# Two heads of the first layer's output projection as a block product in seven parts

## What is computed

```python
h_q = (rmsnorm(layernorm(x)) @ w_q.T).reshape(8, 128, 32, 128)   # 32 heads of 128
h_k = (context @ w_k.T).reshape(8, 128, 32, 128)
h_v = (context @ w_v.T).reshape(8, 128, 32, 128)
score = softmax(einsum("bqhd,bkhd->bhqk", h_q, h_k) + position_bias, masked)
attn = einsum("bhqk,bkhd->bqhd", score, h_v).reshape(8, 128, 4096)
x = x + tanh(gate) * (layernorm(x) + attn @ w_out.T)
```

## Time and profile before

| what | value |
|---|---|
| runs | 1004.22, 1004.27, 1004.35 us |
| the profiled execution: its time, its span | 1004.49 us, 1002.7 us |
| PE, DVE, ACT, POOL busy | 99%, 47%, 41%, 34% of the span |
| one group, from output projection to output projection | 105.1 us |
| output projection, all groups | 768 matmuls of 512 columns, 180.6 us busy |

### The profile page before, as it was taken

How to read it: one execution, slowest core, us unless ns; L and a number is a source line. 1 busy time by engine, 2 the same in 40 slices (tenths; PEclk the granted TensorE clock), 3 DMA queues, 4 the chain that set the end, 5 groups by cost and what they waited for, 6 DMA issues and landing times.

```text
span 1002.7 us, 14920 instructions
## 1 busy us (share of the span) xinstructions
PE 995.0 (99%) x5204; PEld 844.5 (84%) x5204; DVE 466.8 (47%) x957; ACT 413.2 (41%) x1110; POOL 336.4 (34%) x317
## 2 busy tenths in 40 slices
PE   8999999999999999999999999999999999999998
PEld 7888888888888888888888888888888888888885
DVE  5654622462155305532364235622462287766664
ACT  6563233432453244334442344234432454555630
POOL 3351414122330424041414051314122333587640
PEclk9999999999999999999999999999999999999999
DMA  8021111101110201010111011111101103300002
GB/s 312 22 84 55 42 43 64 32 21 63 42 52 0 84 28 55 10 63 21 63 31 63 21 63 31 42 42 63 31 21 64 42 2 99 122 33 1 1 1 84
DMA packets 16402, 50.52 MB, mean 50 GB/s; under 512 B 3056, under 2 KB 3312, under 8 KB 15600
## 3 DMA queue, kind: packets, MB, share of 16 engines
q1 hardware_dynamic: 15360, 48.75, 14.2%
q10 hardware_dynamic: 1008, 1.32, 0.4%
HBM read 47.97 MB, written 2.10 MB: 50 GB/s over the span
## 4 chain that ended last, share of the span: by engine, by line
PE 97%; DVE 1%; ACT 1%; POOL 1%; DMA 0%; issue 0%; SPq 0%; ACTq 0%; DVEq 0%
PE bank L1311 34%; PE bank L1369 17%; PE bank L1323 17%; PE bank L1430 10%; PE bank L1333 6%; PE bank L1353 6%; PE bank L1344 3%; PE bank L1423 2%; PE bank L1570 1%; PE bank L1507 1%; PE bank L1527 1%; POOL wvo L362 1%; DMA craw<-in_ctx 0%; DVE xt L891 0%; PE bank L1256 0%
## 5 line engine op out<-in xcount | busy, mean ns | idle before, releaser
L1311 PE MATMUL bank<-xt,wq 128*128 128x512 f32 x768 | 186.4, 393 | 0.0
L1311 PE MATMUL bank<-ct,wk 128*128 128x512 f32 x768 | 181.6, 392 | 0.7 <-DVE ct L857 0.7
L1369 PE MATMUL bank<-wvo,ao 128*128 128x512 f32 x768 | 180.6, 392 | 0.0
L1323 PE MATMUL bank<-wvo,ct 128*128 128x512 f32 x768 | 178.1, 390 | 0.2 <-POOL wvo L362 0.2
L1323 PEld LDWEIGHTS bank<-wvo,ct 128*128 128x128 f32 x768 | 143.4, 188 | 29.9 <-POOL wvo L362 0.6
L1311 PEld LDWEIGHTS bank<-ct,wk 128*128 128x128 f32 x768 | 142.7, 188 | 30.0 <-DVE ct L857 1.3
L1311 PEld LDWEIGHTS bank<-xt,wq 128*128 128x128 f32 x768 | 142.4, 188 | 29.1
L1369 PEld LDWEIGHTS bank<-wvo,ao 128*128 128x128 f32 x768 | 142.4, 188 | 28.6
L362 POOL TENSOR_TENSOR wk<-stage,wk 128x512 fp32r<-128x512 f32 x32 | 41.9, 1310 | 295.9 <-ACT wk L553 295.9
L362 POOL TENSOR_TENSOR wvo<-stage,wvo 128x512 fp32r<-128x512 f32 x64 | 81.7, 1306 | 162.3 <-ACT wvo L553 162.3
L569 ACT ACTIVATE prob<-prob,nmax 128x128 f32<-128x128 f32 x256 | 99.2, 389 | 61.5 <-DVE nmax L922 61.5
(11 more groups left out here) (148 smaller groups left out, 1120.1 us busy)
## 6 DMA issues: line engine op xcount, KB each, us to landing
stage<-in_w SPq DMA_DIRECT2D x63, 512.0 KB, 3.3
xraw<-in_x SPq DMA_DIRECT2D x2, 1024.0 KB, 12.5
bias<-in_bias SPq DMA_DIRECT2D x8, 256.0 KB, 2.7
cs<-in_ctx SPq DMA_DIRECT2D x1, 2048.0 KB, 9.2
out<-acc SPq DMA_DIRECT2D x8, 256.0 KB, 2.1
craw<-in_ctx ACTq DMA_DIRECT2D x4, 256.0 KB, 6.2
craw<-in_ctx SPq DMA_DIRECT2D x4, 256.0 KB, 6.5
stage<-in_w_key SPq DMA_DIRECT2D x1, 1024.0 KB, 4.8
```

The costliest lines, as they stand in the source:

```text
L1311: mm = pe.matmul(bank[un_of[first][u] % RING][:, :], w[:, i, c, :], t[:, j, c, half(s)], start=(c == 0 and i + j == 0), stop=(c == KC - 1 ...
L1323: mm = pe.matmul(bank[un_of[first][u] % RING][:, :], ct[:, i, c, b * P:(b + 1) * P], wvo[:, j, c, :], start=(c == 0 and i + j == 0), stop= ...
L1369: mm = pe.matmul(bank[to][:, :], ao[:, h, i, b * P:(b + 1) * P], wvo[:, j, h, :], start=(h == heads[0] and i + j == 0), stop=(h == heads[- ...
```

## The change

The output projection no longer works on single heads. Two heads (pair "a" is heads 0 and 1, pair "b" heads 2 and 3) form the inner dimension of a block product with 2 by 2 blocks: token tiles 0 to 3 or 4 to 7, first or second head, output columns 0 to 255 or 256 to 511. It is done with 7 products of sums of blocks (P1, P7, P2, P4, P6, P3, P5, in this order) in place of 8. A product is 4 token tiles by 3 passes with 256 columns, in two units of 6 matmuls. Each product is summed over all groups in its own accumulator (accp, 7 of them), and the seven are combined once, after the last group, to acc. The accumulators take the start values of x before the first group.

```diff
-CHUNKS = ["k0", "q0", "v0", "v1", "v2", "v3", "k1", "q1", "o0", "o1", "o2", "o3", "k2", "q2", "k3", "q3"]
+CHUNKS = ["k0", "q0", "v0", "v1", "v2", "v3", "k1", "q1", "o0", "o1", "k2", "q2", "k3", "q3", "o2", "o3"]
+NPROD = 7
+P1, P7, P2, P4, P6, P3, P5 = range(NPROD)
-    bm = place("bm", [P, 2, B, P], fp32)
+    bm = place("bm", [P, B, P], fp32)
-    ao = place("ao", [P, GH, 2, TOK], fp32r)
+    yb = place("yb", [P, NPROD, 2, D], fp32r)
...
+                def product(g, m, pair, *ks):
+                    n = 2 * g + "ab".index(pair)
+                    for k in ks:
+                        pe.wait_ge(s_olo, n * NPROD + k + 1)
+                        if k in (P1, P2, P4):
+                            pe.wait_ge(s_yv, n * 8 + {P1: 1, P2: 3, P4: 4}[k])
+                        else:
+                            pe.wait_ge(s_ylo, n * 4 + {P7: 1, P6: 2, P3: 3, P5: 4}[k])
+                        for t in range(2):
+                            u = f"{pair}{k}{t}"
+                            bank_free(g, u, m)
+                            for b in range(2):
+                                tile = (2 * t + b) * P
+                                for i, j in PASSES:
+                                    mm = pe.matmul(bank[un_of[m][u] % RING][:, b * 256:b * 256 + 256], yb[:, k, i, tile:tile + P],
+                                                   wo[:, k, j, :], start=(i + j == 0), stop=(i == 1))
+                            mm.then_inc(s_unit, 1)
```

```diff
+                    proj(g, "k", 1, 0, m)
+                    proj(g, "k", 1, 1, m)
+                    proj(g, "q", 1, 0, m)
+                    transposes(g, 0, m)
+                    proj(g, "q", 1, 1, m)
+                    attend(g, 0, m)
+                    scores(g, 1, m)
+                    proj(g, "k", 2, 0, m)
+                    proj(g, "k", 2, 1, m)
+                    product(g, m, "a", P1)
+                    proj(g, "q", 2, 0, m)
+                    transposes(g, 1, m)
+                    product(g, m, "a", P7)
+                    proj(g, "q", 2, 1, m)
+                    attend(g, 1, m)
+                    scores(g, 2, m)
+                    proj(g, "k", 3, 0, m)
+                    proj(g, "k", 3, 1, m)
+                    product(g, m, "a", P2)
+                    proj(g, "q", 3, 0, m)
+                    product(g, m, "a", P4)
+                    transposes(g, 2, m)
+                    if last:
+                        proj(g, "q", 3, 1, m)
+                        attend(g, 2, m)
+                        scores(g, 3, m)
+                        product(g, m, "a", P6, P3, P5)
+                        product(g, m, "b", P1)
+                        transposes(g, 3, m)
+                        product(g, m, "b", P7)
+                        attend(g, 3, m)
+                    else:
+                        product(g, m, "a", P6)
+                        proj(g, "q", 3, 1, m)
+                        product(g, m, "a", P3)
+                        attend(g, 2, m)
+                        product(g, m, "a", P5)
+                        scores(g, 3, m)
+                        proj(g, "k", 4, 0, m)
+                        proj(g, "k", 4, 1, m)
+                        product(g, m, "b", P1, P7)
+                        transposes(g, 3, m)
+                        proj(g, "q", 4, 0, m)
+                        attend(g, 3, m)
+                        proj(g, "q", 4, 1, m)
+                    product(g, m, "b", P2, P4, P6, P3, P5)
```

The sums of blocks on both sides are new work. POOL forms four sums of output weight blocks per pair (out_sum) and seven low parts of 256 columns (out_lo), with ACT's seven high parts (out_hi); POOL also makes the low parts of four sums of attended values (left_lo). DVE makes the sums from PSUM:

```diff
+                def biasmask(g, h, ahead=False):
...
+                    n = g * 2 * GH + (2 * GH if ahead else 2 * h)
+                    pool.wait_ge(s_sadd, n + 2)
...
+                def left_first(g, pair):
+                    left_low(g, pair, P1, 1, 0)
+                    dve.wait_ge(s_yhi, g * 16 + 8 * pair + 2)
+                    dve.tensor_tensor(ydiff[:, :], bank[6][:, :], ydiff[:, :], ALU.subtract).then_inc(s_yv, 1)
+                def left_sums(g, pair):
+                    n = g * 16 + 8 * pair
+                    dve.tensor_tensor(yraw[:, P6, 1, :], bank[7][:, :], ydiff[:, :], ALU.subtract).then_inc(s_yv, 1)
+                    dve.wait_ge(s_yv, n + 5)
+                    dve.tensor_tensor(yraw[:, P3, 1, :], bank[6][:, :], yraw[:, P6, 1, :], ALU.subtract).then_inc(s_yv, 1)
+                    dve.tensor_tensor(yraw[:, P5, 1, :], yraw[:, P6, 1, :], yb[:, P1, 0, :].bitcast(fp32), ALU.add).then_inc(s_yv, 1)
+                    dve.wait_ge(s_yv, n + 7)
+                    dve.tensor_tensor(yraw[:, P5, 1, :], yraw[:, P5, 1, :], yb[:, P1, 1, :].bitcast(fp32), ALU.add).then_inc(s_yv, 1)
```

The orders of ACT, POOL and DVE around head 2, and of DVE at the end of the last group:

```diff
+                    left_second(g, 0)
+                    exps(g, 2, range(2))
+                    for k in (P6, P3, P5):
+                        left_hi(g, 0, k)
+                    empty(g, "k3a", m)
+                    empty(g, "k3b", m)
...
+                    left_lo(g, 0, P7)
+                    biasmask(g, 2)
+                    w_lo(g, "k3", m)
+                    w_lo(g, "q3", m)
+                    biasmask(g, 3)
+                    for k in (P6, P3, P5):
+                        left_lo(g, 0, k)
+                    out_sum(g, 1, P7, m)
+                    out_lo(g, 1, P1, m)
+                    out_lo(g, 1, P7, m)
...
+                    left_second(g, 0)
+                    softmax_in(g, 2)
+                    if last:
+                        dequant(3)
+                    left_sums(g, 0)
+                    softmax_out(g, 2, 0)
+                    softmax_out(g, 2, 1)
+                    add_out(g, m, "a", P2, P4)
...
+                    left_sums(g, 1)
+                    add_out(g, m, "b", P2, P4, P6)
+                    if last:
+                        combined(accp[:, P6, :, :], accp[:, P6, :, :], accp[:, P1, :, :], "b41")
+                        combined(acc[:, 0:HB, 0:256], accp[:, P1, :, :], accp[:, P2, :, :], "b41")
+                    add_out(g, m, "b", P3)
+                    if last:
+                        combined(accp[:, P3, :, :], accp[:, P3, :, :], accp[:, P6, :, :], "b51")
+                        combined(accp[:, P7, :, :], accp[:, P7, :, :], accp[:, P6, :, :], "b51")
+                    add_out(g, m, "b", P5)
```

```diff
+                x1(0)
+                stats1(0, 0)
+                x1(1)
+                stats1(1, 0)
+                combined(acc[:, HB:B, 0:256], accp[:, P7, :, :], accp[:, P4, :, :], "b61")
+                dve.wait_ge(S["comb"], 5)
+                x1(2)
+                x1(3)
                 dve.wait_ge(s_rows, 16)
                 for row, g in ((R_FFN, 2), (R_BASE, 3)):
                     dve.tensor_scalar(rows[:, row, :], rows[:, row, :], tg[:, g:g + 1], None, ALU.mult).then_inc(S["rows"], 1)
+                key(0)
                 stats1(2, 0)
+                key(1)
                 stats1(3, 0)
                 lo(0, 0)
```

More of the change, by code:

```diff
@@ L683, in _ @@
+                    if last:
+                        for c in range(2, KC):
+                            act.wait_ge(s_scaled, c + 1)
+                            split_hi("key", c)
+                    else:
+                        for j in range(1, GH):
+                            w_hi(g, f"w{j}", m)
+                body(0, "first")
                 with act.Fori(1, LAST) as g:
-                    group(g, False)
-                group(LAST, False, last=True)
+                    body(g, "loop")
@@ L1403, in group @@
-                    for b in range(4):
-                        project(g, f"o{b}", [0, 1, 2])
-                    transposes(g, GH - 1)
-                    for b in (4, 5):
-                        project(g, f"o{b}", [0, 1, 2])
-                    attend(g, GH - 1, first)
-                    for b in (6, 7):
-                        project(g, f"o{b}", [0, 1, 2])
-                    for b in range(B):
-                        project(g, f"p{b}", [GH - 1], b if last and b >= HB else None)
```

881 lines of the change are left out of this document (533 added, 348 removed).

## The result

The changed kernel takes 1051.1 us (median of 4 runs, 1050.1 to 1053.1) against 1004.3 before: 1.047 times as long, 95% interval 1.045 to 1.049. The forecast was 1024, with a range of 995 to 1052. The profiled run took 1050.05, its span 1047.8.

A forecast was written before the change was run, and what follows sets the result against it. The prediction took PE, busy 99% of the span, to bound the kernel. 1004.5 - 12.8 + 15.2 + 1.8 + 2.2 + 13.1 = 1024.0, and 1023.8 against the median: 1024 us, range 995 to 1052.

The forecast's parts named there:

- the port of POOL and DVE: Rival: two-input SBUF operations of DVE and POOL shut each other out; 1045 by turns, 1070 otherwise; chance 0.20.
- Saved on PE: Output projection in every group: seven products for 96 matmuls of 512 columns save 1.6 us a group, 12.8 in all.
- Softmax of heads 1 and 2: Every group: DVE's sign change waits under POOL's mask, so banks for queries empty late; 1.9 x 8 = 15.2 us.
- a kept run: Port rival's worse case: POOL keeps its run of low parts, 5 us a group and 8 at the combinations: 1070.
- End of a group: P6 waits for attend 3, ACT's emptying, a high part and a POOL low part; 0.25 x 7 = 1.8 us.
- First group: ACT's copies stand behind POOL's mask and small parts, so scores 1 wait; 2.2 us, bounds 1 and 3.5.
- Last group and tail: Five waits from the last group's dequantization to the tail's first tiles; together 13.1 us, bounds 7 and 16.
- (a): Last group: a dequantization step on DVE stands between maximum and left sums, delaying head 3's queries; 2.3 us.
- (b): Last group: DVE needs 13.6 us before attend 3's second half, PE's own work 10.7; 2.9 us.
- (c): Last group: DVE's 6.1 us before a bank for P6, against 3.8 of attend and products; 2.0 us with a restart.
- (d): Start of tail: POOL's key low parts, 5.1 us, stand behind the last left low part; 2.7 us.
- (e): Tail: DVE's adds, combinations and statistics end 3.2 us behind PE's three key tiles.

The follow-up runs named there:

- turns: Changed kernel, POOL waiting for head 2's scaled probabilities before the low parts of P6, P3 and P5; saved 0.60 us a group.
- dequant2: Changed kernel, last group's four dequantization parts spread out, the first two to where DVE was idle; last stretch gained 2.4 us.
- mask: Changed kernel, POOL adding mask and bias only once both maxima of the head before are negated; saved 0.74 us a group.
- all2: Changed kernel with the mended orders of start, first group, loop groups, last group and tail together; 1014.8 us, 1.010 times before.
- all3: all2 with ffn low parts later, head 3's transposed probabilities copied by ACT, and POOL's head 2 mask held for head 1's scaled probabilities; 1011.9 us.
- free: Changed kernel, POOL waiting for head 2's scaled probabilities, then low parts of P6, P3, P5, with head 3's mask last; 1056.9 us.
- all4: all3 with POOL's four ffn low parts behind the norms of token tiles 0 and 1, without their own wait; 1012.4 us, 1.0075 times before.
- tail: Changed kernel, POOL forming the four ffn low parts before those of the last pair's P6, P3, P5; gained 5 to 6 us.
- tail2: Changed kernel, two key low parts before the last pair's P6, row vectors' transfer ahead, key tile 0 emptied earlier; gained 5 to 6 us.
- ptact: all2 with ACT instead of DVE copying head 3's transposed probabilities in the last group; 1.0094 times before.
- fill: Changed kernel with unread products of 512 columns keeping PE busy in two long tail waits; median 1.3 us lower.

## Why the forecast was right in sign and too small

The direction and the range held; the sum came to 19.7 us over before, and the kernel lost 46.8. That the range held is in part luck: two steps worth 17 us were left out of the sum, and its upper bound came from the port's rival, not from the waits that did come. These two failed: **the port of POOL and DVE, put at 0** (9 us measured in P4's gaps alone), and **every wait priced as its gap, with nothing for the granted clock behind it** (7.7 us). By the prediction's steps:

- **Saved on PE, 12.8.** Nearly right: free of waits a group is 1.13 to 1.49 shorter, 9 to 12 in all. The spacing of 256 columns is 0.122 (36 matmuls in 4.54) against 0.120, so the row was the better guide than the 109 ns of the Trainium skill ("TensorE: Matmul & The Clock Gate", section "Back-to-back issue gap").
- **Softmax of heads 1 and 2, 15.2.** Mechanism and place right, size 11: q3a 1.3 for 1.5, query half 2a 0.1 to 0.3 for 0.4.
- **The port, 0 in the sum.** The alternation with POOL costs 1.3 before P4's second unit in seven of the eight groups, 9 in all, and turns shows that it is this: with POOL's run held back the gap is gone. (In the last group q3a's longer wait seems to cover it: in dequant2, where q3a waits 1.4, the gap is there too.) It also lengthened the combinations (2.0 and 2.3 for 1.2) and held the start values. The rival priced it at 2.2 by turns and 5 by a kept run; the measured value is below both; PE had waited 1.3 at q3a just before and so asked later, which fits but wasn't tried by itself. Its sign for the port (a period above 108, scalings of 2 us and more) was too coarse: they took 1.74, and the period was 106.75. By its own terms the kept run comes to 1072, not 1070. The prediction named the half microsecond on which it hung and took the favourable side. The Trainium skill ("SBUF — State Buffer", section "Who interferes with whom") has the rule, and for an operation with a scalar between SBUF buffers too, where it runs in a mode that uses both ports. The runs agree: a sum of two SBUF inputs took 1.86 for 0.68, a scaling 1.74 for 0.69, the negation 1.74 for 0.17, while in mask the sum ahead (L1239, one input a bank) kept its 0.69 inside POOL's 2.4. No run shows in which mode the negation and the scalar steps ran.
- **End of a group, 1.8.** Nothing there.
- **First group, 2.2.** Exactly the gap (2.17). Missed: the start values, put at 0 "unless POOL holds them", which it did (2.7 and more), and the clock behind the gap (1.7).
- **Last group and tail, 13.1.** (a) right: q3a 3.6 is the loop's 1.3 and 2.3. (b) 2.9 against 1.2 + 0.8 + 1.0 = 3.0. (c) 2.0 against 0.7 + 1.7. (d) 2.7 against 5.0, because POOL's parts took 6.95 for 5.1 beside the combinations. (e) 3.2 against 5.8; the 2.8 over is the rows' transfer, behind another wait in SP's queue, which the step took as landed. Then P7's second unit 1.5, not seen.
- **Not in the sum at all: the granted clock.** Four falls, 1.7 + 1.6 + 1.9 + 2.5 = 7.7 us in the trace.

1024 + 9 (port) + 7.7 (clock) + 3 (start values) + 5 (d and e) + 1.5 (P7) - 4 (softmax) - 1.8 (end of a group) comes to 1044. The other 7 are not assigned one by one: 1 to 4 are missing from the saving on PE, and the start scatters by 2. What stays open is the 17 us of the last group in its best order. DVE is busy there (all2) from 834.5 to 883 with no pause over 0.2 us, and POOL is idle in some 11 of these 49 us, so DVE's row of steps is the likelier bound; how much either would give if its work were less was tried only for 1.3 us.

## What to carry to other kernels

Price a wait on a full PE as gap plus what the clock takes behind it, and follow every in-order queue past a moved wait, ACT's and SP's too: one copy waiting in front of a full bank was worth 27 us. Where two engines share a port, move all their overlaps at once; the mask moved alone mostly changed its victim. A saving of 1.5 us a group needs more groups than 8 to pay for a last group that nothing follows: by all3's 17.9 us there and 1.49 a group, an estimate is 12 groups before it.

## What the runs showed of the hardware

The granted clock fell to half behind waits that were short, and the length of the wait doesn't decide it alone. By the idle time in brackets it fell behind 2.01, 3.48, 4.83 and 5.68 us in the changed kernel and held behind 1.57 and less. But in free it fell behind a wait of 2.65 us in three of six groups and held in the other three, in turn, with the same work before each. At the same place and after the same work it held behind 2.35 us in all3 and fell behind 2.31 in all4:

```profile
850.53 4.54 PE L1748 MATMUL bank<-wvo,yb 128*128 128x256 f32 x36 [2.35 <-DVE accp L1277]
850.52 6.02 PE L1747 MATMUL bank<-wvo,yb 128*128 128x256 f32 x36 [2.31 <-POOL yb L458]
```

In tail it held behind 3.38 us, between two falls (36 matmuls in 8.45). Behind two waits close together, of 1.4 to 1.5 and 0.8 us, the twelve matmuls that follow took 4.58 in tail2 and in ptact, and 2.98 in all2. With PE kept busy by unread products (fill) it held both times, though 2.6 us of the second wait were left.
